# A graph layer on one core: x in two float32r parts instead of three bf16, with the counts as the stationary side

## The reference

```python
h = node_features @ W_node.T + b_node
e = edge_features @ W_edge.T + b_edge
msg = h[src] + e
msg = msg @ W_msg.T + b_msg
s = jax.ops.segment_sum(msg, dst, num_segments=n)
deg = jax.ops.segment_sum(jnp.ones(dst.shape, msg.dtype), dst, num_segments=n)
out = _layernorm(x + s / jnp.maximum(deg, 1.0)[:, None], axis=-1)
```

## Time and profile before

| | us |
|---|---|
| median of 3 runs | 787.46 |
| lowest, highest | 785.98, 790.88 |
| span of the profiled execution | 779.9 |
| PE busy | 693.2 |
| DVE busy | 629.4 |
| ACT busy | 438.5 |
| POOL busy | 276.4 |

### The profile page before, as it was taken

The page is one execution under the profiler, slowest core; times in us unless marked ns, Lnnn a source line. Parts: engine busy times, 40 slices in busy tenths (PEclk is TensorE's granted clock), DMA queues, the critical chain, the costliest instruction groups (busy, mean ns, idle before and its releaser), DMA issues.

```text
span 779.9 us, 24842 instructions
## 1 busy us (share of the span) xinstructions
PE 693.2 (89%) x10360; PEld 624.6 (80%) x10360; DVE 629.4 (81%) x1155; ACT 438.5 (56%) x897; POOL 276.4 (35%) x210
## 2 busy tenths in 40 slices
PE   3355577989999989999999998999999999999995
PEld 3244466878989979999998997989999999989994
DVE  7889896868998858888888877688898888879722
ACT  3322396656566546656666564556666666656641
POOL 2737300301434825526526455443443542000000
PEclk9975598999999989999999998999999999999998
DMA  5953543534565555575472476455655665554000
GB/s 174 320 184 75 126 135 113 180 116 137 172 211 193 188 184 187 174 247 187 146 265 79 162 275 205 139 165 200 220 195 182 202 214 179 172 183 169 17 15 16
DMA packets 81518, 130.71 MB, mean 168 GB/s; under 512 B 12100, under 2 KB 25126, under 8 KB 81303
## 3 DMA queue, kind: packets, MB, share of 16 engines
q1 hardware_dynamic: 73230, 115.79, 44.4%
q0 software_dynamic: 7200, 12.39, 5.7%
q10 hardware_dynamic: 974, 0.90, 0.5%
HBM read 125.80 MB, written 3.23 MB: 165 GB/s over the span
## 4 chain that ended last, share of the span: by engine, by line
PE 70%; DVE 18%; issue 5%; POOL 2%; DMA 2%; ACT 1%; DVEq 1%; ACTq 0%; POOLq 0%
PE x_ps L745 39%; PE count_ps L730 14%; PE win_ps L666 11%; DVE key_hot L886 3%; DVE row_hot L886 3%; PE win_ps L673 3%; DVE onehot L852 2%; POOL x_gathered L607 2%; PE misc_ps L761 1%; DMA x_gathered<-in_x_dram,x_index 1%; PE misc_ps L762 1%; DVE region L959 1%; DVE place L858 1%; DVE past L907 1%; DVE x_gathered L988 1%
## 5 line engine op out<-in xcount | busy, mean ns | idle before, releaser
L1416 ACT CAST region<-count_ps 128x490 bf16<-128x490 f32 x575 | 324.5, 574 | 196.8 <-PE count_ps L730 191.1
L745 PE MATMUL x_ps<-region,x_rest 128*128 128x250 bf16 x2254 | 415.8, 271 | 0.0
L745 PE MATMUL x_ps<-region,x_hi 128*128 128x250 bf16 x1127 | 307.1, 272 | 0.5 <-ACT region L1416 0.5
L607 POOL DMA_INDIRECT x_gathered<-in_x_dram,x_index x144 | 201.0, 1396 | 270.9 <-PE count_ps L730 250.3
L886 DVE TENSOR_TENSOR row_hot<-iota_bf,row 125x3200 bf16<-125x3200 bf16 x115 | 209.4, 1821 | 41.3 <-PE count_ps L730 29.6
L730 PE MATMUL count_ps<-key_hot,row_hot 125*128 125x98 bf16 x2875 | 225.4, 210 | 15.3 <-ACT region L1416 8.6
L745 PEld LDWEIGHTS x_ps<-region,x_rest 128*128 128x128 bf16 x2254 | 212.1, 98 | 16.6
L730 PEld LDWEIGHTS count_ps<-key_hot,row_hot 125*128 125x128 bf16 x2875 | 186.5, 100 | 38.5 <-issue 11.0
L886 DVE TENSOR_TENSOR key_hot<-iota_bf,key 125x2500 bf16<-125x2500 bf16 x115 | 167.2, 1454 | 0.0
L745 PEld LDWEIGHTS x_ps<-region,x_hi 128*128 128x128 bf16 x1127 | 109.8, 97 | 8.3 <-ACT region L1416 0.6
L666 PE MATMUL win_ps<-edges,onehot 128*32 128x128 f32 x3232 | 107.4, 287 | 1.9 <-DMA edges<-in_edge_attr_dram 1.8
(11 more groups left out here) (194 smaller groups left out, 419.0 us busy)
## 6 DMA issues: line engine op xcount, KB each, us to landing
edges<-in_edge_attr_dram SPq DMA_DIRECT2D x101, 1024.0 KB, 7.6
resid<-in_x_dram SPq DMA_DIRECT2D x25, 125.0 KB
out_dram<-y SPq DMA_DIRECT2D x25, 125.0 KB
x_gathered<-in_x_dram,x_index POOLq DMA_INDIRECT x144
region<-in_dst_dram ACTq DMA_DIRECT2D x1, 768.0 KB
win_src<-in_src_dram,clipped_int POOLq DMA_INDIRECT x23, 4.6
x_index<-in_src_dram SPq DMA_DIRECT2D x9, 8.0 KB, 5.7
region<-in_L_gnn_W_node_dram SPq DMA_DIRECT2D x1, 64.0 KB
```

The lines of the kernel that those rows point to most:

```text
L607: pool.indirect_dma_start(out=x_gathered[:, i, :], out_offset=None, in_=x[:, :], in_offset=bass.IndirectOffsetOnAxis(ap=x_index[:, k, i:i ...
L745: mm = pe.matmul(x_ps[m % 2][:, 0:NB], rows, counts[m % 2][:, b, :], start=(n == 0), stop=(n == PARTS - 1))
L1416: act.copy(counts[m % 2][:, :, f * FILL * 2:(f + 1) * FILL * 2], count_ps[fill % COUNT_BANKS][:, 0:FILL * KEYS].rearrange("p (n b) -> p b ...
```

## The change

x is multiplied by its product of weights and given its bias in the prologue, on PE, in 13 chunks of four blocks (`turn_x`, `make_x`), and the result is written by ACT as two float32r parts: `copy_high` writes the value as float32r, `take_high` subtracts that from the exact value in PSUM with a matmul by minus the identity, and `copy_low` writes the rest. `x_step` staggers the three steps, so that a chunk is turned while the one before is multiplied and the one before that is split. The steps stand between the sums of the five lead slots. The splits of POOL are gone. The products of weights are made in lead slot 0, for which `load_small` stands ahead of `load_x` in the queue of SP.

The counts are float32r, in two buffers of 125 nodes. They are now the stationary side, and the two parts of x of a block move, 256 columns: 49 matmuls for each half, 98 for a round. The first half is applied in fills 14 to 24 of its own round, the second in fills 1 to 11 of the next. The bank of fill 12 holds nodes of both halves and is moved in two copies. The sum of a half group has its nodes in partitions and its high and low sums side by side; ACT copies the high one to `group_x` (`take_high`), DVE adds the low one (`take_x`) and, in `add_message`, the edge part (`joined`). `finish_group` of these groups no longer multiplies x, and their bias operations on DVE are gone.

```diff
-        group_x = sb("group_x", [P, 2, NB])
-        x_hi = sb("x_hi", [P, XB, D], BF16)
-        x_rest = sb("x_rest", [P, XB, D])
+        arena = -(-nc.sbuf_base // 32) * 32
         SECOND = -(-N // 16) * 16
         region = sb("region", [P, 2 * SECOND])
-        counts = [region[:, k * SECOND:k * SECOND + XB * NB // 2].bitcast(BF16).rearrange("p (b n) -> p b n", b=XB) for k in range(2)]
+        counts = [nc.alloc_sbuf_tensor_at(f"counts{k}", [P, XB, PB], F32R, offset=arena + 4 * k * SECOND) for k in range(2)]
+        x_raw = sb("x_raw", [P, XB, 2 * D])
+        x_parts = nc.alloc_sbuf_tensor_at("x_parts", [P, XB, 2, D], F32R, offset=arena + 8 * SECOND)
+        sums_e = sb("sums_e", [P, SE_COLS])
+        group_x = sb("group_x", [PB, 2, D])
...
             load_near(0)
-            split_rest(0)
-            split_rest(1)
             load_window(0)
             load_near(1)
-            for i in range(2, 5):
-                split_rest(i)
             load_window(1)
             load_near(2)
-            for i in range(5, 7):
-                split_rest(i)
             load_job(0)
-            for i in range(3):
-                split_low(i)
             load_window(2)
             load_job(1)
-            for i in range(3, 7):
-                split_low(i)
...
+            def turn_x(c):
+                if c == 0:
+                    pe.wait_ge(weights_ready, 1)
+                pe.wait_ge(x_in[0], 16)
+                if c * XCHUNK + XCHUNK > 21:
+                    pe.wait_ge(x_in[1], 32)
+                if c >= 1:
+                    pe.wait_ge(xt_ready, c)
+                for b in range(XB)[chunk(c)]:
+                    j = b - c * XCHUNK
+                    mm = pe.transpose(x_ps[1][:, j * D:(j + 1) * D], x_raw[:, b, 0:D], ident[:, :])
+                mm.then_inc(x_turned, 1)
+
+            def make_x(c):
+                pe.wait_ge(xt_ready, c + 1)
+                if c >= COUNT_BANKS:
+                    pe.wait_ge(x_lo_ready, c - COUNT_BANKS + 1)
+                bank, blocks = chunk_bank(c), range(XB)[chunk(c)]
+                n = len(blocks)
+                pe.matmul(bank[:, 0:n * D].rearrange("p (b d) -> p b d", d=D), ones[0:1, :],
+                          bias_row[0:1, :].rearrange("p (b d) -> p b d", b=1).to_broadcast([1, n, D]), start=True, stop=False)
+                for b in blocks:
+                    j = b - c * XCHUNK
+                    mm = pe.matmul(bank[:, j * D:(j + 1) * D], x_raw[:, b, D:2 * D], w_both[:, 0, :], start=False, stop=(b == blocks[-1]))
+                mm.then_inc(x_made, 1)
+
+            def take_high(c):
+                pe.wait_ge(x_hi_ready, c + 1)
+                n = len(range(XB)[chunk(c)])
+                pe.matmul(chunk_bank(c)[:, 0:n * D].rearrange("p (b d) -> p b d", d=D), minus_ident[:, :], x_parts[:, chunk(c), 0, :],
+                          start=False, stop=True, skip_group_check=True).then_inc(x_less, 1)
+
+            def x_step(i):
+                if i < XCHUNKS:
+                    turn_x(i)
+                if 0 <= i - 1 < XCHUNKS:
+                    make_x(i - 1)
+                if 0 <= i - 2 < XCHUNKS:
+                    take_high(i - 2)
...
-            def apply_counts(m, piece, pieces):
+            def apply_counts(m, h, piece):
                 if piece == 0:
-                    pe.wait_ge(bank_moved, (m + 1) * ROUND_FILLS)
-                    if m == 0:
-                        pe.wait_ge(x_ready, 7)
-                        pe.wait_ge(weights_ready, 1)
-                    elif m >= 2:
+                    pe.wait_ge(bank_moved, m * ROUND_FILLS + (SPLIT + 1 if h == 0 else ROUND_FILLS))
+                    if m == 0 and h == 0:
+                        pe.wait_ge(x_lo_ready, XCHUNKS)
+                        pe.wait_ge(count_taken, NEAR + JOBS)
+                    if m >= 2 and h == 0:
                         pe.wait_ge(x_taken, m - 1)
-                for n in range(PARTS * piece // pieces, PARTS * (piece + 1) // pieces):
-                    b, part = n // 3, n % 3
-                    rows = x_hi[:, b, :] if part == 0 else x_bf[:, b, :, 1 if part == 1 else 0]
-                    mm = pe.matmul(x_ps[m % 2][:, 0:NB], rows, counts[m % 2][:, b, :], start=(n == 0), stop=(n == PARTS - 1))
-                if piece == pieces - 1:
+                for b in range(XB * piece // PIECES, XB * (piece + 1) // PIECES):
+                    mm = pe.matmul(x_ps[m % 2][0:PB, h * 2 * D:(h + 1) * 2 * D], counts[h][:, b, :],
+                                   x_parts[:, b, :, :].rearrange("p k d -> p (k d)"), start=(b == 0), stop=(b == XB - 1))
+                if piece == PIECES - 1:
                     mm.then_inc(x_mm, 1)
 
             def finish_group(n):
                 u, m, i = finishes[n]
                 first = finished[n] * NB
                 pe.wait_ge(added, items_by[u])
-                if m is not None:
-                    pe.wait_ge(x_taken, m + 1)
-                    x_sums = group_x[:, m % 2, :]
-                else:
-                    x_sums = sums_e[:, X_COLS + i * NB:X_COLS + (i + 1) * NB]
                 free_misc()
                 for h in range(2):
                     to = misc_ps[0:PB, FIN + h * D:FIN + (h + 1) * D]
-                    pe.matmul(to, sums_e[:, first + h * PB:first + (h + 1) * PB], w_both[:, 1, :], start=True, stop=False)
-                    mm = pe.matmul(to, x_sums[:, h * PB:(h + 1) * PB], w_both[:, 0, :], start=False, stop=True)
+                    mm = pe.matmul(to, sums_e[:, first + h * PB:first + (h + 1) * PB], w_both[:, 1, :], start=True, stop=(i is None))
+                    if i is not None:
+                        at = X_COLS + i * NB + h * PB
+                        mm = pe.matmul(to, sums_e[:, at:at + PB], w_both[:, 0, :], start=False, stop=True)
                 mm.then_inc(fin_mm, 1)
...
                     if t == 0:
                         pe.wait_ge(count_taken, 2)
                         count_blocks(2)
+                        turn_weights()
+                        make_weights()
                     if t == 1:
                         turn_keys(0)
+                    for i in X_STEPS[t]:
+                        x_step(i)
                     continue
                 m, s = divmod(g, SEGS)
                 for f in range(FILLS):
                     count_fill(g, f)
-                    if m > 0:
-                        apply_counts(m - 1, s * FILLS + f, ROUND_FILLS)
+                    at = s * FILLS + f
+                    if m > 0 and 1 <= at <= PIECES:
+                        apply_counts(m - 1, 1, at - 1)
+                    if at >= ROUND_FILLS - PIECES:
+                        apply_counts(m, 0, at - ROUND_FILLS + PIECES)
...
-            apply_counts(ROUNDS - 1, 0, 2)
             finish_group(GROUPS - 2)
-            apply_counts(ROUNDS - 1, 1, 2)
+            for piece in range(PIECES):
+                apply_counts(ROUNDS - 1, 1, piece)
             finish_group(GROUPS - 1)
...
+            def take_x(m):
+                dve.wait_ge(high_taken, m + 1)
+                low = x_ps[m % 2][0:PB, :].rearrange("p (h k d) -> p h k d", h=2, k=2)[:, :, 1, :]
+                dve.tensor_tensor(group_x[:, :, :], low, group_x[:, :, :], ALU.add).then_inc(x_taken, 1)
+
             def add_message(n):
+                u, m, i = finishes[n]
                 g, k = finished[n], n % 2
                 dve.wait_ge(fin_mm, n + 1)
-                dve.wait_ge(resid_in[k], 16 * (n // 2 + 1))
                 if n >= 2:
                     dve.wait_ge(out_done[k], 16 * (n // 2))
+                from_edges = misc_ps[0:PB, FIN:FIN + 2 * D].rearrange("p (h d) -> p h d", h=2)
+                if m is not None:
+                    dve.wait_ge(x_taken, m + 1)
+                    dve.tensor_tensor(y[:, k, :, :], from_edges, group_x[:, :, :], ALU.add).then_inc(joined, 1)
+                    dve.wait_ge(joined, m + 1)
...
+            def copy_turned(c):
+                act.wait_ge(x_turned, c + 1)
+                n = len(range(XB)[chunk(c)])
+                act.copy(x_raw[:, chunk(c), D:2 * D], x_blocks(x_ps[1], n)).then_inc(xt_ready, 1)
+
+            def copy_high(c):
+                act.wait_ge(x_made, c + 1)
+                n = len(range(XB)[chunk(c)])
+                act.copy(x_parts[:, chunk(c), 0, :], x_blocks(chunk_bank(c), n)).then_inc(x_hi_ready, 1)
+
+            def copy_low(c):
+                act.wait_ge(x_less, c + 1)
+                n = len(range(XB)[chunk(c)])
+                act.copy(x_parts[:, chunk(c), 1, :], x_blocks(chunk_bank(c), n)).then_inc(x_lo_ready, 1)
+
+            def x_step(i):
+                if i < XCHUNKS:
+                    copy_turned(i)
+                if 0 <= i - 1 < XCHUNKS:
+                    copy_high(i - 1)
+                if 0 <= i - 2 < XCHUNKS:
+                    copy_low(i - 2)
...
-                if f == 0 and m == 1:
-                    act.wait_ge(early_done, 1)
```

(32 more changed lines are left out.)

134 lines of the change are left out of this document (68 added, 66 removed).

## The result

The changed kernel takes 766.29 us (766.14 to 768.96), the kernel before 787.7: a ratio of 0.970, 95% interval 0.966 to 0.975. It is 21.4 us faster; 48 were forecast, and the time lies inside the range. The profiled execution has a span of 764.4 us. In every other run of this study the time is about 1.8 us above its span, so the execution of before that was profiled (779.9) took an estimated 781.7, less than any of the four times of before (785.98 to 790.88), and the "7.6 around it" of the forecast was a misreading.

What follows compares the result with a forecast made beforehand. PE was taken to bound the fifteen later rounds, with DVE close behind and setting the prologue. Terms +4 - 7 - 2 - 29 - 3 - 11 = -48 off 787.5 gave 739 us, range 705 to 775.

Steps and rivals of the forecast that it cites:

- 7.6 around it: Whole kernel before: its median 787.46 was taken to hold 7.6 us around the profiled span of 779.9, unchanged by the change.
- Applying the counts: PE, each round: 98 float32r matmuls at 0.111 replace 147 bf16 ones, load hidden, so 5.0 us leave PE.
- rival 1: Counts on PE: weight load hides only partly, 0.125 to 0.165 a matmul, half the rounds' gain lost, 755 to 765; chance 0.10.
- DVE becomes the bound: Rounds: DVE's 25.6 and 27.2 us exceed PE's 21.8 and 24.2, leaving PE idle 3 us in each.
- the total of -29: Fifteen rounds, 285.9 to 720.8 us: 7 x 1.6 + 7 x 2.5, the gather's round gaining 0.
- The prologue: +4: Up to 90.7 us: POOL's splits go (ceiling 25 us back), x is made on PE; +4, bounds -10 and +25.
- -7 in rounds 1 to 3: 90.7 to 190.3 us, the rounds with counting jobs: PE loses work but DVE and ACT carry the jobs; -7 (0 to -15).
- the fills then run from a stock: Prologue: DVE makes hots, counts and weights unstretched while PE makes x; fills after the first, near 74, run at DVE's pace.
- Rival 3: Prologue: the making of x is exposed, 20 to 25 us later, the rest as forecast, 758; chance 0.13.
- Finishing, the end, the gather's rounds: Finishing saves PE 0.45 a round; the end gains 3 and 11 us; gather rounds from 190.3 to 285.9 gain 2.
- Rival 2: Counts on PE: two passes or load in series, 0.22 a matmul, rounds 5.4 us longer, about 904; chance 0.10.
- rival 4: Rounds: DVE is not the bound, rounds fall to 22 to 24 us, -29 becomes up to -75, about 695; chance 0.06.

Runs made afterwards that it cites:

- e7: The changed kernel with counts, parts of x and minus the identity in bf16, third part of x left out; 752.2 us, 0.947 of the kernel before.
- e3: The changed kernel with the counts applied to only 25 of the 49 blocks of x; 748.0 us, 0.939 of the kernel before.
- e4: The kernel before with only the changed kernel's smaller scratch memory for descriptors (4096); 792.3 us, 0.997 of the kernel before.
- e2: The changed kernel with a pair of windows placed after the first fill of a slot, not the second; 762.2 us, 0.959 of the kernel before.
- e11: The changed kernel with key_hot made for the first two slots only, so DVE has less work; 746.3 us, 0.941 of the kernel before.
- e12: The kernel before without POOL's subtractions, the first part of x standing in for all three; 783.1 us, 0.990 of the kernel before.
- e6: The changed kernel without the making of x, ACT writing zeros into the parts instead; 752.3 us, 0.947 of the kernel before.
- e1: The changed kernel with the two counts that start the counting jobs moved from round 0 into lead slots 2 and 3; 765.9 us, 0.962 of the kernel before.
- e9: The changed kernel with earlier job starts, placing after the first fill and a short float32r bias matmul together; 740.2 us, 0.935 of the kernel before.
- e10: The changed kernel with earlier job starts, earlier placing, short bias matmul, and counts and parts in bf16; 727.5 us, 0.918 of the kernel before.

## Why the prediction was wrong in size

*Applying the counts: 0.111 a matmul.* This step failed. It is 0.118 in a stream and 0.20 for the first of a piece: 49 matmuls in 11 pieces are 5 x 0.68 + 6 x 0.56 = 6.8, 13.5 a round, 0.138 each; 2.4 us came off PE where 5.0 were counted. That is rival 1 by its price. That the time too came out near its 755 to 765 (given 0.10), and inside the range, is in part luck: rival 1 loses about half of the gain in the rounds and nothing else, and half of what is missing lies in rounds 1 to 3. e7 shows that the type makes it, and since bf16 does the same columns at 0.112, that it is not the columns. The Trainium skill, TensorE: Matmul & The Clock Gate, section Weight-path perf modes, whose rule the forecast set aside, gives the fast weight load to 128 weights of a type that is not FP32 and does not name float32r. The listed loads agree in direction (0.190 on average for float32r of 125 columns, 0.098 for bf16 of 128 before). But by that rule the 125 bf16 columns of e7 get no fast load either: they are listed at 0.14, longer than the 0.112 between their matmuls, and cost next to nothing there. So neither the rule nor the earlier trace rows decides it, and how a load of either length is hidden no run here separates.

*DVE becomes the bound: 25.6 and 27.2, on average 26.4.* This step failed too. As DVE's own work the average is right: with PE relieved, rounds are 24.3 and 28.2 (e7), on average 26.3, and 23.3 and 28.8 at a granted clock of 1.00 (e3), 26.1. The two kinds were exchanged: the waits at 609 to 621 us in the earlier trace rows, 2.89 in all, lie in the round from 607.20 to 634.44, which is the one of 27.24. With that, the same sum gives 24.7 and 28.1, and the total of -29 stays. But PE, not DVE, goes on setting the rounds: it waits 1.0 us for DVE in all fifteen, and the forecast's PE idle for 3 us in each does not appear. PE's round is 26.55 and 27.99, not 21.8 and 24.2. Of the 4.8 us between in a round of two pairs, 2.7 are the counts applied (with 0.3 of waiting at the fill of two copies), 1.8 the sums and 0.3 the fills; of the 3.8 with three pairs, 2.9, 0.6 and 0.3.

The sums are a term that the forecast put at nothing, as nothing was changed in them. Some of it was there before: e4 has up to 0.8 of the 1.8, and the profile that the forecast was read from has none. The other 1.1 us go when placing comes one fill earlier (e2) and when DVE has less to do (e11), in the second pair of sums both times. So the order of the two engines bears on it, but the profile shows nothing that PE waits for there, and why its matmuls come late stays open. On average a round is 27.3; DVE's work alone needs at most 26.3 (e7), PE's at most 26.6 (e11). 14 rounds x 0.8 are the 11 us missing in the fifteen rounds.

*The prologue: +4, and -7 in rounds 1 to 3.* Each half of the account was near: without the splits the keys of round 1 come 16 us earlier (e12; the ceiling was 25), and the making of x takes 22 to 25 (e6; 30 on PE were worked out, for 74 as the first fill, and it came at 80), which gives the measured +7.8. Part of the 80 is that the first chunks ran at half the rate, 4.9 us each. What failed is "the fills then run from a stock", together with -7 for rounds 1 to 3: before, DVE's slow round 0 (36 us from the first fill to the keys of round 1; 18 after) covered the gathers of the counting jobs. Now the pairs of edges are wanted while these gathers run, and PE waits 8 us (8.2 in e6, and 5.1 in e12). e1 moves the gathers ahead and the wait goes, as in e9 and e10; what in the transfers makes the edges late no run separates. That is the greater part of the 16.2 us missing here, not all of it: without the wait, rounds 1 to 3 still take 99.9 (e1) and 96.9 (e9), where 99.6 were before and some 93 forecast. PE waits 9.3 us for ACT's moves of counts in them (8.6 before); what holds them beyond that stays open. Rival 3 (20 to 25 us later, 758) named the size and not the place.

*Finishing, the end, the gather's rounds.* As forecast: -13.2 against -14 at the end, -1.2 against -2 in rounds 4 to 6. Rival 2 did not come, and rival 4 neither: PE stayed the bound, but its rounds did not fall to 22 to 24.

The chances put faster at 0.85, which held; the likeliest case was counted too favourably, since two rivals that were each given about 0.1 came in part and together. The 739 also took a saving read from the profile of 779.9 off a median that stands 7.6 above it.
